# Second attention pass of a graph network: two buffers of turned one-hots, their products taken amid a half, the block ends spread over the turn; the loads of the first loop ahead of x's

## What is computed

```python
def _L0_gnn_ref(x, edge_row, edge_col, edge_val, W, b):
    gathered = edge_val[:, None] * x[edge_col]
    support = jax.ops.segment_sum(gathered, edge_row, num_segments=N)
    ...
def _gat_layer(x, src, dst, W, a_src, a_dst, b, num_nodes):
    h = (x @ W).reshape(num_nodes, H, C)
    al_s, al_d = ...
    logits = jax.nn.leaky_relu(al_s[src] + al_d[dst], 0.2)
    alpha = _segment_softmax(logits, dst, num_nodes)
    msg = h[src] * alpha[:, :, None]
    out = jax.ops.segment_sum(msg, dst, num_segments=num_nodes)
...
x = _layernorm(x + _L0_gnn_ref(x, src, dst, edge_weight, ...))   # sums by source
x = _layernorm(x + _L1_gnn_ref(...))   # _gat_layer with 4 heads, then _gat_layer with 1 head of 64
x = _layernorm(x + _L2_gnn_ref(...))
x = _layernorm(x + _L3_gnn_ref(...))   # three layers
```

## Time and profile before

| what | value |
|---|---|
| median of 3 runs | 8321.05 us (8319.97 to 8323.98) |
| profiled execution: its own time / its span | 8319.94 us / 8315.2 us |
| busy: PE, DVE, ACT, POOL | 72%, 43%, 19%, 69% |
| set-up, until the barrier | 0 to 83.4 us |
| first loop's scatters (784) | first at 134.0, last at 1591.8 us |
| first attention pass, gathers (784) | first at 2080.0, last at 3069.0 us |
| second attention pass, gathers (784) | first at 3133.6, last at 4201.6 us |
| four passes over the edges that follow | 4259 to 8315 us |
| mean granted TensorE clock | 0.791 of full |

### The profile page before, as it was taken

How to read it: one execution, slowest core, us unless ns; L and a number is a source line. 1 busy time by engine, 2 the same in 40 slices (tenths; PEclk the granted TensorE clock), 3 DMA queues, 4 the chain that set the end, 5 groups by cost and what they waited for, 6 DMA issues and landing times. The chain is left out here.

```text
span 8315.2 us, 131640 instructions
## 1 busy us (share of the span) xinstructions
PE 6005.0 (72%) x30082; PEld 4650.2 (56%) x30082; DVE 3537.5 (43%) x13640; ACT 1568.6 (19%) x5156; POOL 5771.3 (69%) x5577
## 2 busy tenths in 40 slices
PE   3777777672788876777766666677777777777777
PEld 1444444471555555666645555566666666656665
DVE  3444444352666655555543333222222222233333
ACT  2333333220122221222212222100000000000000
POOL 3888888502777756777757777577776777767776
PEclk9888888786999995555568899788877887777777
DMA  8777777532444433333334444344443444434443
GB/s 258 115 115 115 114 114 114 101 117 76 109 116 117 116 94 81 80 80 80 80 81 118 117 119 117 94 117 118 118 117 108 118 117 118 118 106 117 117 119 107
DMA packets 530468, 925.51 MB, mean 111 GB/s; under 512 B 134408, under 2 KB 362170, under 8 KB 527802
## 3 DMA queue, kind: packets, MB, share of 16 engines
q0 software_dynamic: 330704, 676.12, 35.5%
q1 hardware_dynamic: 199658, 248.23, 9.5%
HBM read 731.08 MB, written 192.85 MB: 111 GB/s over the span
## 5 line engine op out<-in xcount | busy, mean ns | idle before, releaser
L711 PE MATMUL bank<-onehots,rows 128*128 128x128 f32 x12544 | 2507.8, 347 | 937.7 <-DMA rows<-gcn_rows,index 577.9
L711 PEld LDWEIGHTS bank<-onehots,rows 128*128 128x128 f32 x12544 | 2058.4, 240 | 1380.2 <-DMA rows<-gcn_rows,index 745.2
L655 POOL DMA_INDIRECT rows<-gcn_rows,index x2352 | 2233.9, 950 | 816.3 <-issue 653.8
L1127 POOL DMA_INDIRECT rows<-gat_rows,index x1568 | 1512.0, 964 | 666.4 <-issue 455.4
L1449 POOL DMA_INDIRECT support<-rows,index x784 | 1215.1, 1550 | 285.9 <-DMA support<-rows,index 140.3
L1259 PE MATMUL bank<-onehots,rows 128*128 128x128 f32 (+1 forms) x4704 | 932.7, 335 | 414.3 <-DVE rows L1333 414.3
L1259 PEld LDWEIGHTS bank<-onehots,rows 128*128 128x128 f32 (+1 forms) x4704 | 702.5, 200 | 627.2 <-issue 330.4
L655 POOL DMA_INDIRECT rows<-norm,index x784 | 742.8, 947 | 295.1 <-issue 223.9
L742 DVE TENSOR_SCALAR onehots<-iota,half_offset,edge_values 128x128 f32<-128x128 f32 x3136 | 854.4, 360 | 169.2 <-issue 96.7
L752 DVE TENSOR_TENSOR acc<-acc,bank 128x256 f32 x396 | 165.1, 417 | 1352.6 <-PE bank L711 1352.6
L1535 PE MATMUL cross_bank<-same_source,onehots 128*128 128x128 f32 x1568 | 373.3, 326 | 435.8 <-DVE same_source L1591 435.8
(11 more groups left out here) (279 smaller groups left out, 6353.6 us busy)
## 6 DMA issues: line engine op xcount, KB each, us to landing
dst_row<-in_dst_flat SPq DMA_DIRECT2D x100, 512.0 KB
source_row<-in_src_flat SPq DMA_DIRECT2D x99, 512.0 KB, 5.0
rows<-gcn_rows,index POOLq DMA_INDIRECT x2352, 2.8
support<-zeros POOLq DMA_DIRECT2D x16, 1632.0 KB, 32.9
support_rows<-support SPq DMA_DIRECT2D x40, 640.0 KB, 7.2
rows<-gat_rows,index POOLq DMA_INDIRECT x1568, 2.7
gcn_rows<-out SPq DMA_DIRECT2D x150, 128.0 KB
own_rows<-gcn_rows SPq DMA_DIRECT2D x150, 128.0 KB
```

The costliest lines, as they stand in the source:

```text
L655: nc.gpsimd.indirect_dma_start(rows[:, k, :], None, table, bass.IndirectOffsetOnAxis(ap=index[:, k:k + 1], axis=0),).then_inc(gathered[k], 16)
L711: done = nc.tensor.matmul(by_chunk(banks[h])[:, c, :], rows[:, k, c * P:(c + 1) * P], onehots[:, k, :], start=first and c == 0, stop=final ...
L1127: nc.gpsimd.indirect_dma_start(rows[:, k, :], None, table, bass.IndirectOffsetOnAxis(ap=index[:, k:k + 1], axis=0),).then_inc(gathered[k], 16)
```

## The change

In the attention pass: `from_window` gets two buffers, and `turned_onehots` of a half waits for the shares of the half before the last one, not of the last. The shares of the next half are multiplied after tile 3 of each half instead of ahead of tile 0. `pe_third` moves from after tile 4 to after tile 2. On DVE, `dve_late` moves from behind batch 1 to behind `turned_onehots(i, 3)`, and `dve_later` to the end of the turn; on ACT, `act_late` moves from behind batch 1's exponentials to behind `act_clear`. The first pass runs the same code, without shares, and with empty `dve_late` and `dve_later`.

In the first loop: the loads of `x_window` and `source_row` come first. x is loaded in five pieces of ten blocks, and these, the five stores to `scratch` and the two stores out of set-up are issued one behind the loads of each of the first 12 turns. The wait for them stands behind the loop. Set-up no longer stores, and its SP no longer waits.

```diff
@@ -1094,7 +1094,7 @@
...
             window_share = sbuf("window_share", [P, 2, heads])
-            from_window = sbuf("from_window", [P, HALF, P])
+            from_window = sbuf("from_window", [P, 2, HALF, P])
             share_banks = [psum(f"share_bank{h}")[:, 0:HALF * heads].rearrange("p (k h) -> p k h", h=heads)
@@ -1193,11 +1193,11 @@
...
                     exponentials(i, 1)
-                    if late is not None:
-                        ends.act_late(act, s, late)
                     exponentials(i, 2)
...
                         ends.act_clear(act, s, b, zeros)
+                    if late is not None:
+                        ends.act_late(act, s, late)
                     exponentials(i, 3)
@@ -1236,14 +1236,13 @@
...
                     for k in range(HALF):
-                        done = nc.tensor.matmul(share_banks[h][:, k, :], from_window[:, k, :],
+                        done = nc.tensor.matmul(share_banks[h][:, k, :], from_window[:, h, k, :],
                                                 window_share[:, h, :], start=True, stop=True)
...
                     if first:
-                        shares(i, h + 1)
@@ -1264,7 +1263,9 @@
...
                         multiply(i, k)
-                        if late is not None and k == 4:
+                        if k % HALF == BATCH - 1:
+                            shares(i, k // HALF + 1)
+                        if late is not None and k == 2:
                             ends.pe_third(pe, s, late)
@@ -1312,10 +1313,10 @@
...
                     dve.wait_ge(row_loaded[n % 2], i * 16 + 16 * (n // 2 + 1))
-                    if not (isinstance(i, int) and 2 * i + n < 1):
-                        dve.wait_ge(s.shared, i * 2 + n)
-                    nc.vector.tensor_scalar(from_window[:].rearrange("p k e -> p (k e)"), dst_row[:, n % 2, :],
+                    if not (isinstance(i, int) and 2 * i + n < 2):
+                        dve.wait_ge(s.shared, i * 2 + (n - 1))
+                    nc.vector.tensor_scalar(from_window[:, n % 2, :, :].rearrange("p k e -> p (k e)"), dst_row[:, n % 2, :],
                                             g.window_lane[:, bass.ds(i * 2 + n, 1)], None, ALU.is_equal
@@ -1355,18 +1356,18 @@
...
                     batch_of(i, 1)
-                    if late is not None:
-                        ends.dve_late(dve, s, late)
                     batch_of(i, 2)
...
                     if late is not None:
-                        ends.dve_later(dve, s, late)
+                        ends.dve_late(dve, s, late)
                     if b is not None:
...
                     batch_of(i, 3)
+                    if late is not None:
+                        ends.dve_later(dve, s, late)
@@ -1457,18 +1458,20 @@
...
             def _(sync):
-                kept = 0
+                later, fifth = [], g.blocks // 5
                 if first_pass:
-                    sync.dma_start(g.x[:], g.x_dram.rearrange("(b p) f -> p b f", p=P)).then_inc(s.kept, 16)
-                    kept += 16
+                    x_rows = g.x_dram.rearrange("(b p) f -> p b f", p=P)
+                    later += [(g.x[:, b:b + fifth, :], x_rows[:, b:b + fifth, :]) for b in range(0, g.blocks, fifth)]
                     for n, dram in scratch.items():
...
                             to = min(at + zeros.shape[1], g.tiles * n)
-                            sync.dma_start(target[:, at:to], zeros[:, 0:to - at]).then_inc(s.kept, 16)
-                            kept += 16
-                with sync.Fori(0, g.tiles // RING) as i:
+                            later.append((target[:, at:to], zeros[:, 0:to - at]))
+                    later += [(g.half_offset_dram[:], g.half_offset[:]),
+                              (g.half_base_float_dram[:], g.half_base_float[:])]
+                def loads(i):
                     for h in range(2):
@@ -1482,8 +1485,13 @@
...
-                if first_pass:
-                    sync.wait_ge(s.kept, kept)
+                for i, (out, in_) in enumerate(later):
+                    loads(i)
+                    sync.dma_start(out, in_).then_inc(s.kept, 16)
+                with sync.Fori(len(later), g.tiles // RING) as i:
+                    loads(i)
+                if later:
+                    sync.wait_ge(s.kept, 16 * len(later))
                 sync.wait_ge(s.matrices, g.tiles + HALF)
@@ -1697,7 +1705,7 @@
...
         with phase(nc, "loaded", "iota", "own", "relu", "added", "gated", "kept",
-                   "turned", "wide", "stored", "zeros_ready") as (block, s):
+                   "turned", "wide", "zeros_ready") as (block, s):
             @block.sync
@@ -1714,11 +1722,6 @@
...
                                    ).then_inc(s.loaded, 16)
-                sync.wait_ge(s.kept, 1)
-                sync.dma_start(g.half_offset_dram[:], g.half_offset[:]).then_inc(s.stored, 16)
-                sync.dma_start(g.half_base_float_dram[:], g.half_base_float[:]).then_inc(s.stored, 16)
-                sync.wait_ge(s.stored, 32)
             @block.gpsimd
...
```

## The result

Over 6 runs each the changed kernel took a median of 8285.31 us (8278.15 to 8289.43), the kernel before 8320.85 (8318.70 to 8323.98): a ratio of 0.9957, 95% interval 0.9946 to 0.9968. It is faster by 35.5 us, 0.43%, where 76 were forecast: less than half. The time lies 0.7 us inside the upper end of the range, 8286. The profiled execution took 8287.14 us, its span 8285.1, 30.1 us under that of before (8315.2).

What follows compares the result with a forecast made beforehand. POOL was taken to bound the first loop, a chain through DVE and PE the second attention pass. Terms -1 - 28 + 6 - 48 - 5 summed to -76, forecasting 8245 us, range 8203 to 8286.

Steps and rivals of the forecast that it cites:

- Set-up: Set-up: removing SP's wait releases nobody; only 392 KB leave the way of the zeros, -1 us.
- Start of the first loop: Ahead of the first scatter: source_row lands by 92, spare is late next, DVE starts at about 96; -28 us.
- In the first loop: Scatters beside the moved DMAs: three large pieces stall a scatter 2.1 us each, the rest hidden; +6 us, bounds 0 and 29.
- The rival of an expensive first loop: First loop gives back what its start gained, engines being 75% busy: +29 instead of +6, 8268 us; chance 0.08.
- Second pass, the removed waits: Second attention pass: DVE's waits go, POOL's pitch binds, 30 us of long records stay; gathers 1016 us, -52.
- Second pass, what is late next: Second pass: a ring through shares and dst_row reload, about 20.7 us, is level with POOL; gathers -48 instead of -52.
- The ring rival: Second pass: the ring binds at 21.4 us a turn, no gain at the end, total -43, 8278 us; chance 0.20.
- Second pass, its end: Behind the second pass's last gather: batch 3 follows the gather's landing by 2 us; -5 us, bounds -7 and 0.
- First pass: First attention pass: pe_third moves into time PE waits anyway, act_late behind a copy, POOL at its pitch; 0 us.
- the best case: Whole kernel: clock rises or POOL alone sets the pace, pieces cost nothing; -120, 8201 us; as a rival, chance 0.12.
- the first three rivals: Whole kernel: ring binds (8278, chance 0.20), all goes well (8201, 0.12), first loop gives back its start's gain (8268, 0.08).
- the fourth: Second pass: the waits only change place, the change not doing what it says; -23, 8298 us; chance 0.05.

Runs made afterwards that it cites:

- the ring cut: Changed kernel, but SP waits for the shares only ahead of window_share's load, so dst_row reloads earlier: 8232.3 us, 0.9896 of before.
- the changed pass by itself: Kernel before the change with only attention_pass taken from the changed kernel: 8292.8 us, 0.9968 of before.
- small pieces, later: Changed kernel with x in 25 pieces, zeros a quarter as wide, each piece issued four tiles later: 9602.7 us against 9711.5 before, 0.9898.
- the kernel of all parts and later pieces: Changed kernel with early dst_row reload, x whole at the start, zeros in quarters, pieces four tiles later: 0.9828, 0.9788 and 0.9799 of before.

## Why the prediction was right or wrong

**Set-up (-1)**: right. `spare` is issued at 82.29 instead of 83.82.

**Start of the first loop (-28)**: right, step by step: `spare` was what came late next, DVE started at 95.7 against "about 96", the first scatter stood at 105.6.

The forecast fell short by 40 us in the median (35.5 of 76). In the profile, where 46 are missing, three terms hold 40 of them: the first loop 13, the second pass's gathers 22, its end 5.

**In the first loop (+6, bounds 0 and 29)**: wrong, 19 to 27. The step that failed is "`source_row` of the next half is issued half a turn, 15 us, behind a piece, so it does not queue behind it". It looked at the load behind the piece and not at the one ahead: in the code a piece goes out directly after `loads(i)`, half a microsecond behind the second `source_row`. The 1.7 us that a scatter has to spare was worked out for a quiet loop and spent once on `source_row` (the 8 gaps in before show that it just about suffices) and a second time on the piece. So even the pieces that the prediction took "as hidden" were paid: in the changed kernel's profile the gaps over 2.0 us behind the four pieces of x in the loop sum to 7.6 us over the pitch, those behind the five stores of zeros to 10.1 (in the three other profiles of this loop 7 to 10 and 10 to 15); cut to quarters, the zeros cost no less than whole. The rival of an expensive first loop had the size nearly right (+29), and its reason wrong, as far as the comparison across chips carries: not the engines' share of 75% but the place. That its number was near is luck. The 10 us that I estimated by the rule in the Trainium skill (DMA: Bandwidth & Descriptors, Queues, rings and completion order) were nearer than my 6 and still about half; the page itself gives no such figure, and no run here isolates the rule. Cutting the zeros' rows to a quarter brought no gain (1469.5 and 1470.8), so these runs don't show the length of rows as the cause.

**Second pass, the removed waits (-52)**: right as a mechanism, and too small: with the ring cut, gathers took 992.5 where 1016 was forecast (-75). The long records were not fixed at 30 us; they came to 15. A slip of 3 us stands beside it: 989.0 is 15 over 974, not 12, so that the sum should have been 1019.

**Second pass, what is late next (-48 instead of -52)**: wrong, -25.7. The step named the right kind of thing and followed the wrong half. It went through the reload behind the second half's shares, found 21.4 by durations, 20.7 start to start, and called that level with POOL. That reload in truth landed with time to spare, also because the shares ahead of it ran in 1.84 in that turn (at 3598.24), and in 2.0 in the median of the pass, and not in the 3.41 of the earlier trace rows that were counted for both halves. The ring that binds goes from the first-half shares through the reload for the second half and then through DVE's whole work from batch 3 to the block end, 10.73 us, of which the forecast counted 2.6. Two facts were to be had: DVE works in one fixed order, so everything between L1319 of one half and the division lies in the ring; and batch 2 needs the shares that now come four tiles later. The ring rival's price (turn 21.4, total -43, 8278) was nearly the result; it had 0.20. Its turn fits by luck in part, since it was added up along the other ring, and its total still has +6 for the first loop. I took the lower of two values for its length because PE's modelled durations overlap, and had no row for a ring's slack.

**Second pass, its end (-5)**: wrong in the changed kernel, where the wait of 4.79 for the shares stands in the last turn too and the next pass's first gather follows after 57.4 us (57.6 before the change). It came, some -5.5, as soon as the reload was early.

**First pass (0)**: right, 989.9 against 989.0.

**Of what would show it wrong**, two of five came true clearly: L1319 waiting for `dst_row` (107.9 us), a scatter stretch longer by more than 15 us (18.7). Turns stood at 21.3 in the mean, a little under the 21.4 named there, and `pe_third` waited for `left` 1.2 us at most. The first attention pass took 989.9 against 989.

Two sentences of the prediction on its numbers don't add up: the range is said to start at the best case, 8203, and that case is worked out as 8201; and 0.90 for "faster" is the forecast and the first three rivals alone, without "most of the fourth".

## What to carry to other kernels

When shares of work are moved later in a loop, follow each buffer's refill back to what releases it, for each half separately, and through the whole in-order program of every engine on the way; a refill that waits for more than the reader of its own buffer (here SP's common wait for two loads) closes a ring that nobody needs.

Background transfers in a loop that runs at its own pitch cost, in these runs, between nothing and all of their bytes depending on where in the turn they were issued: try them where no other load has just gone out, and in pieces shorter than the slack of one iteration.

## What the runs showed of the hardware that was not expected

Three of the chips took 9711 to 9798 us for the kernel that takes 8320 on the others, with the same median durations (within 2 ns) of all frequent operations up to the end of the first loop. What differs comes after it. From 2100 to 3000 us (columns as in the earlier trace rows) and PE's own waits, first on a chip at 8320 (the changed pass by itself), then on one at 9711 (small pieces, later); both run the same code there:

```profile
2100.00:3000.00 900.00, 790.31 (x5102) 536.90 (x5102) 599.41 (x2114) 182.56 (x926) 674.83 (x714) 0.99 0.44 115
```

```profile
PE bank L1258 <- DVE rows L1334: 133.9, 127, 26.1
```

```profile
2100.00:3000.00 900.00, 740.05 (x4124) 494.50 (x4124) 480.32 (x1704) 149.86 (x760) 551.17 (x582) 0.86 0.36 94
```

```profile
PE bank L1258 <- issue: 99.1, 102, 2.7
```

PE stands still 102 times, up to 2.7 us, with nothing to wait for that the profile shows, and the granted clock is 0.86 instead of 0.99 there. Why these chips do it no run here shows. The kernels also compare differently there: the kernel of all parts and later pieces is at 0.979 to 0.983 of before there, where without the later pieces it was 0.989 on a chip at 8320. Chip and pieces differ at once, so this gain is put down to neither.

And 6.4 MB sent out in the 20 us before the first scatter delayed it by 0.5 to 3 us and took up to 4 us more from the scatters right behind it, while the DMA engines' share in the loop, 0.75, looked like room and was none at the wrong moment.
